# Attention: GpSimd multiplies and adds from ScalarE's copies, and the value products are placed three items apart

## The reference

```python
def _L0_attn_b_ref(x, w_in, w_out):
    # B = 4, L = 1024, E = 128, H = 16 heads, D = 8
    qkv = jnp.einsum('ble,fe->blf', x, w_in)
    q, k, v = to_heads(...)                       # [B, H, L, D]
    scores = jnp.einsum('bhqd,bhkd->bhqk', q, k) / sqrt(D) + alibi_bias(H, L)   # causal
    attn = jax.nn.softmax(scores, axis=-1)
    ctx = jnp.einsum('bhqk,bhkd->bhqd', attn, v)
    return jnp.einsum('ble,fe->blf', ctx, w_out)
x = x + _L0_attn_b_ref(_layernorm(x), w_in, w_out)
```

## Time and profile before

| | before |
|---|---|
| median of 3 runs | 1679.25 us (1678.73 to 1680.9) |
| the profiled execution's own time | 1676.88 us |
| its span in the profile | 1675.1 us |
| busy over the span: PE, DVE, ACT, POOL | 98%, 76%, 63%, 15% |
| attention, units 0 to 15 | 724.19 to 1128.87 us |
| one unit with g of 1 to 3 | 24.12 us |
| one unit with g = 0 (4, 8, 12) | 27.42 us |

### The profile page before, as it was taken

How to read it: one execution, slowest core, us unless ns; L and a number is a source line. 1 busy time by engine, 2 the same in 40 slices (tenths; PEclk the granted TensorE clock), 3 DMA queues, 4 the chain that set the end, 5 groups by cost and what they waited for, 6 DMA issues and landing times.

```text
span 1675.1 us, 28454 instructions
## 1 busy us (share of the span) xinstructions
PE 1636.6 (98%) x10387; PEld 1170.9 (70%) x10387; DVE 1272.8 (76%) x2541; ACT 1063.6 (63%) x1976; POOL 248.1 (15%) x469
## 2 busy tenths in 40 slices
PE   6999999999999999999999999999999999999998
PEld 4668787887778887754444544438888888888887
DVE  6789677776877777789999999946666666666665
ACT  6555765675566565578888888885555555555554
POOL 6522001200210113421211221220000000000000
PEclk9999999999999999999999999999999999999999
DMA  7000011002000023223212111100000000000000
GB/s 226 1 0 1 1 30 34 1 1 55 12 1 1 25 90 113 89 83 97 63 28 65 46 47 52 28 3 1 7 1 7 1 7 7 1 7 7 1 7 7
DMA packets 63446, 52.46 MB, mean 31 GB/s; under 512 B 7999, under 2 KB 58574, under 8 KB 63310
## 3 DMA queue, kind: packets, MB, share of 16 engines
q1 hardware_dynamic: 63136, 50.57, 10.4%
q10 hardware_dynamic: 174, 0.07, 0.0%
HBM read 32.40 MB, written 18.22 MB: 30 GB/s over the span
## 4 chain that ended last, share of the span: by engine, by line
PE 89%; DVE 6%; ACT 3%; issue 1%; POOL 0%; DMA 0%; DVEq 0%; SPq 0%; POOLq 0%
PE ps L1380 7%; PE ps L1417 7%; PE ps L1418 7%; PE ps L1419 7%; PE ps L1251 7%; PE ps L1252 6%; PE ps L1253 6%; PE ps L1196 6%; PE ps L933 4%; PE ps L1441 4%; PE ps L1442 4%; PE ps L1443 3%; PE ps L1267 3%; PE ps L1269 3%; PE ps L1268 3%; PE ps L1179 3%
## 5 line engine op out<-in xcount | busy, mean ns | idle before, releaser
L2392 DVE SCALAR_TENSOR_TENSOR hid<-sg,ps 128x512 f32<-128x512 f32 x256 | 175.7, 686 | 183.7 <-PE ps L1419 182.9
L1848 ACT ACTIVATE sg<-ps 128x512 f32<-128x512 f32 x256 | 153.3, 599 | 236.2 <-PE ps L1419 234.6
L1762 ACT ACTIVATE sg<-ps 128x512 f32<-128x512 f32 x256 | 153.4, 599 | 200.3 <-PE ps L1253 195.1
L2254 DVE TENSOR_TENSOR hid<-sg,ps 128x512 f32<-128x512 f32 x256 | 174.8, 683 | 136.9 <-PE ps L1253 95.8
L2244 DVE TENSOR_REDUCE negp<-ps 128x1 f32<-128x512 f32 (+2 forms) x450 | 243.3, 611 | 8.2 <-PE ps L1179 6.8
L1757 ACT ACTIVATE pr<-ps 128x512 f32<-128x512 f32 x384 | 206.4, 601 | 48.1 <-PE ps L1171 30.5
L1251 PE MATMUL ps<-xn_hi,w_hi 128*128 128x512 f32 x510 | 209.1, 410 | 0.0
L1417 PE MATMUL ps<-xn_hi,w_hi 128*128 128x512 f32 x512 | 202.5, 395 | 0.0
L1418 PE MATMUL ps<-xn_lo,w_hi 128*128 128x512 f32 x512 | 200.2, 391 | 0.0
L1252 PE MATMUL ps<-xn_lo,w_hi 128*128 128x512 f32 x510 | 199.8, 392 | 0.0
L1253 PE MATMUL ps<-xn_hi,w_lo 128*128 128x512 f32 x510 | 199.7, 392 | 0.0
(11 more groups left out here) (293 smaller groups left out, 3068.7 us busy)
## 6 DMA issues: line engine op xcount, KB each, us to landing
qs<-qd SPq DMA_DIRECT2D x60, 96.0 KB
ks<-kd SPq DMA_DIRECT2D x60, 96.0 KB
kd<-qkp SPq DMA_DIRECT2D x14, 256.0 KB, 2.9
qd<-qkp SPq DMA_DIRECT2D x7, 384.0 KB, 2.6
w_raw<-in_Wg SPq DMA_DIRECT2D x4, 512.0 KB, 7.3
w_raw<-in_Wu SPq DMA_DIRECT2D x4, 512.0 KB, 7.4
w_raw<-in_Wd SPq DMA_DIRECT2D x4, 512.0 KB, 8.9
work<-hd SPq DMA_DIRECT2D x8, 256.0 KB, 5.0
```

## The change

VectorE keeps only the reciprocal of each result, and now takes it from SBUF. ScalarE copies the transposed result from bank 7 to a new buffer `rt` (nine columns of each 32, so 144 per partition). GpSimd multiplies it into `ctxt`. In the units with g = 0 ScalarE also copies each projection from bank 7 to `yS`, and GpSimd adds that to x. Bank 7 is given free by ScalarE's copies. The last results and the last projections, those of unit 15 and sequence 3, stay with VectorE. The value products get other items, three apart where they were two to five apart, and transposes, copies and projections move with them.

```diff
-VALUES_AT = [10, 13, 15, 18, 23, 26, 29, 33, 35, 38]
+VALUES_AT = [11, 14, 18, 21, 24, 26, 29, 32, 38, 41]
...
-OWN_MAXIMA, BEFORE_T, NEXT_MAXIMA, OWN_T = 4, 7, 29, 32
-CONTEXT_T, PROJECT_OUT = (15, 21), (18, 26)
-BEFORE_OUT, OWN_COPY, PLACE, NEXT_COPY, OWN_OUT = 4, 5, 18, 29, 29
-CONTEXT_OUT = (15, 24)
+OWN_MAXIMA, BEFORE_T, NEXT_MAXIMA, OWN_T = 5, 8, 29, 35
+CONTEXT_T, PROJECT_OUT = (14, 24), (17, 27)
+BEFORE_OUT, OWN_COPY, PLACE, NEXT_COPY, OWN_OUT = 5, 6, 19, 29, 29
+CONTEXT_OUT = (14, 24)
+BEFORE_RESULT, OWN_RESULT = 9, 35
 BEFORE_NORM, OWN_NORM = 10, 35
-PROJECT_ADD = (18, 26)
+PROJECT_COPY = (17, 27)
...
+            def weighted_result(n, c):          # GpSimd
+                g0, at = n % NG * HG * HD, n * 2 + 1 - c
+                pool.wait_ge(T["onorm"], at + 1)
+                g.tensor_tensor(ctxt[...], rt[:, :, :, 0:HD], rl[:]...to_broadcast([P, SUB, HG, HD]),
+                                ALU.mult).then_inc(T["ctx"], 1)
+            def add_projection(b, u):           # GpSimd
+                pool.wait_ge(T["c_out"], projections_out(b, u))
+                g.tensor_tensor(rows, rows, yS[:], ALU.add).then_inc(T["xadd"], 1)
...
             for n in range(UNITS):
                 split_max(n * 2 + 1)
...
+                else:
+                    weighted_result(n - 1, 0)
                 for st in MASKED:
                     mask_step(n, st)
+                    if after_context and st == SUB:
+                        add_projection(b - 1, 0)
...
                         split_max(n * 2 + 2)
+                        if after_context:
+                            add_projection(b - 1, 1)
+                if n < LAST_UNIT:
+                    weighted_result(n, 1)
...
+                def result_to_tokens(n, c):     # ScalarE, after the exponential of item 9 or 35
+                    act.wait_ge(T["oT"], at + 1)
+                    a.copy(rt[:], bank(7)...[:, :, :, 0:HD + 1]).then_inc(T["o_out"], 1)
+                def projection_out(b, u):       # ScalarE
+                    act.wait_ge(T["proj"], b * 2 + u + 1)
+                    a.copy(yS[:], bank(7)).then_inc(T["c_out"], 1)
...
+                def reciprocals(n, c):          # VectorE, after the reduction of item 10 or 35
+                    dve.wait_ge(T["o_out"], tokens_out(at))
+                    v.reciprocal(rl[:], rt[:, :, :, HD]).then_inc(T["onorm"], 1)
...
-                            normalise(n - 1, 0)
-                        if g == 0 and n and k in PROJECT_ADD:
-                            add_projection(b - 1, PROJECT_ADD.index(k))
+                            reciprocals(n - 1, 0)
```

More of the change, by code:

```diff
@@ L129, in reduced_to, with results_out, tokens_out, contexts_out @@
     return EARLY_REDUCES + (n - 1) * REDUCES_TO[-1] + (REDUCES_TO[k] if k >= 0 else 0)
+def results_out(at):
+    return 2 * at + 1 if at < 2 * UNITS - 1 else 2 * at
+def tokens_out(at):
+    return 2 * at + 2
+def contexts_out(b, u):
+    return 4 * b + 2 * u + 1 if b < B - 1 else 4 * b + u + 1
+def projections_out(b, u):
+    return 4 * b + 2 * u + 2
 def jobs_done(n, k):
     return N_JOBS + (n - 1) * NG_S + k + 1
-VALUES_AT = [10, 13, 15, 18, 23, 26, 29, 33, 35, 38]
+VALUES_AT = [11, 14, 18, 21, 24, 26, 29, 32, 38, 41]
 for _sl, _at in enumerate(VALUES_AT):
@@ L433, in build @@
             rl = sb("rl", [P, SUB, HG], F32, two)
+            rt = sb("rt", [P, SUB, HG, HD + 1], F32, two)
         qkd = [nc.dram_tensor(n, (len(PAIRS), D, TOK), BF16, kind="Internal").ap() for n in ("qd", "kd")]
@@ L906, in mask_step @@
                                 pattern=[[0, HG], [1, HALF]], channel_multiplier=-1).then_inc(T["masked"], 1)
+            def weighted_result(n, c):
+                g0, at = n % NG * HG * HD, n * 2 + 1 - c
+                pool.wait_ge(T["onorm"], at + 1)
+                g.tensor_tensor(ctxt[:, c * SUB:(c + 1) * SUB, g0:g0 + HG * HD].rearrange("p t (h d) -> p t h d", h=HG),
+                                rt[:, :, :, 0:HD], rl[:].unsqueeze(3).to_broadcast([P, SUB, HG, HD]),
+                                ALU.mult).then_inc(T["ctx"], 1)
+            def add_projection(b, u):
+                pool.wait_ge(T["c_out"], projections_out(b, u))
+                rows = xs(b * BLK + u * SUB, SUB)
+                g.tensor_tensor(rows, rows, yS[:], ALU.add).then_inc(T["xadd"], 1)
             def norm_of_tile(t):
@@ L915, in _ @@
                     root_of_projected(LAST)
+                else:
+                    weighted_result(n - 1, 0)
+                b, after_context = n // NG, n and n % NG == 0
                 for st in MASKED:
                     mask_step(n, st)
+                    if after_context and st == SUB:
+                        add_projection(b - 1, 0)
                     if n == 0 and st == SUB + 1:
@@ L1392, in context_T @@
                     pe.wait_ge(T["ctx"], b * (2 * NG) + 2 * NG)
-                    if u == 1:
+                    if u == 1 and b < B - 1:
+                        pe.wait_ge(T["c_out"], projections_out(b, 0))
+                    if u == 1 and b == B - 1:
                         pe.wait_ge(T["xadd"], b * 2 + 1)
@@ L1398, in project_out @@
                 def project_out(b, u, to=7):
-                    pe.wait_ge(T["c_out"], b * 2 + u + 1)
+                    pe.wait_ge(T["c_out"], contexts_out(b, u))
                     for j in range(SUB):
@@ L1475, in project_last @@
                         w = slice(2 * D, 3 * D)
-                        pe.wait_ge(T["ctx"], 2)
+                        pe.wait_ge(T["o_out"], tokens_out(1))
                         for j in range(SUB):
@@ L1494, in unit @@
                             if n:
-                                pe.wait_ge(T["ctx"], n * 2 - 1)
+                                pe.wait_ge(T["o_out"], tokens_out(n * 2 - 2))
                             else:
@@ L1512, in unit @@
                             elif g == 0:
-                                pe.wait_ge(T["xadd"], b * 2)
+                                pe.wait_ge(T["c_out"], projections_out(b - 1, 1))
                             else:
-                                pe.wait_ge(T["ctx"], n * 2)
+                                pe.wait_ge(T["o_out"], tokens_out(n * 2 - 1))
                             if n == 1:
@@ L1835, in context_out @@
                     a.copy(ctxT[:], bank(at)).then_inc(T["c_out"], 1)
+                def result_to_tokens(n, c):
+                    at = n * 2 + 1 - c
+                    act.wait_ge(T["oT"], at + 1)
+                    if at:
+                        act.wait_ge(T["ctx"], at)
+                    a.copy(rt[:], bank(7).rearrange("p (t h w) -> p t h w", t=SUB, h=HG)[:, :, :, 0:HD + 1]
+                           ).then_inc(T["o_out"], 1)
+                def projection_out(b, u):
+                    act.wait_ge(T["proj"], b * 2 + u + 1)
+                    if b * 2 + u:
+                        act.wait_ge(T["xadd"], b * 2 + u)
+                    a.copy(yS[:], bank(7)).then_inc(T["c_out"], 1)
                 def input_out(t, at):
@@ L1890, in unit @@
                             place_values((n + 1) // NG, (n + 1) % NG)
+                        if k == BEFORE_RESULT and n:
+                            result_to_tokens(n - 1, 0)
+                        if g == 0 and n and k in PROJECT_COPY:
+                            projection_out(b - 1, PROJECT_COPY.index(k))
                         if g == 0 and n and k in CONTEXT_OUT:
@@ L1896, in unit @@
                             result_out(n, 1)
+                        if k == OWN_RESULT and n < LAST_UNIT:
+                            result_to_tokens(n, 1)
                         if k == LAST_INPUT and n == LAST_UNIT:
@@ L2338, in normalise @@
                     dve.wait_ge(T["oT"], at + 1)
+                    dve.wait_ge(T["ctx"], UNITS * 2 - 2)
                     v.reciprocal(rl[:], src[:, :, :, HD]).then_inc(T["onorm"], 1)
@@ L2347, in add_projection @@
                 def add_projection(b, u, at=7):
+                    dve.wait_ge(T["xadd"], TILES - 2)
                     dve.wait_ge(T["proj"], b * 2 + u + 1)
@@ L2448, in unit @@
                                 dve.wait_ge(G["third"], TILES * 2)
-                            normalise(n, 1)
+                            if n < LAST_UNIT:
+                                reciprocals(n, 1)
+                            else:
+                                normalise(n, 1)
                 def ffn_alone():
```

7 lines of the change are left out of this document (4 added, 3 removed).

## The result

The changed kernel takes 1669.72 us (median of 4 runs, 1668.14 to 1670.63), the kernel before 1678.99 beside it (4 runs): a ratio of 0.9945, 95% interval 0.9927 to 0.9962, or 9.3 us less. A second batch of five runs gave 1669.21 against 1678.87, ratio 0.9943 [0.9931, 0.9956].

What follows compares the result with a forecast made beforehand. VectorE was taken to set the pace in ten ordinary units. Terms 9.2 + 3.7 + 0.7 + 0.3 = 13.9 off 1676.88 gave 1663.0, plus 2.4 for the median 1665.4 us; range 1661.0 to 1673.0.

Steps and rivals of the forecast that it cites:

- the 0.66 a unit: VectorE, both results of a unit: 0.33 us removed between reciprocal and next reduction, twice, 0.66 in all.
- rival E: Slower: GpSimd late with the maxima's split if its multiplication takes 3 us or more; 1686 at 3.5 us; chance 0.05.
- Ten ordinary units: Units 2, 3, 5, 6, 7, 9, 10, 11, 13, 14: from 24.11 to 23.2 us, ten times 0.92, 9.2 in all.
- VectorE idles 0.1 at item 27 and nowhere else: In an ordinary unit under the new places, VectorE's only idle time is 0.1 us, giving a unit of 23.2.
- the walk: An ordinary unit followed item by item, each job no sooner than the reduction three before it: VectorE idle 0.1 us.
- rival B: TensorE or ScalarE takes VectorE's place in ordinary units: gain of 3 to 10 us, middle 7, 1672; chance 0.18.
- the maxima's way back: Maxima through DRAM into the queries, 3.2 us from ScalarE's copy to item 0: cost 0, up to 0.5 with g = 0.
- Units 4, 8, 12: Units with g = 0: from 27.42 to 26.2 us with VectorE idle about 3.05, saving 3.7 over three units.
- The 2.4 that was added for the median: The median of runs lies 2.4 us above the profiled execution, so 1663.0 became 1665.4.
- C (more): Units 4, 8 and 12 gain the full 1.86 each, the reciprocal costs 0.1: 18 us in all, 1661; chance 0.05.
- D (no difference): VectorE's saved time returns in full as idle time because TensorE sets the pace: 1676 to 1682; chance 0.06.
- the wait at item 35: VectorE waiting for ScalarE's copy at item 35: forecast cost 0, at most 0.3 us a unit; rival B allowed 0.3.

Runs made afterwards that it cites:

- the kernel without the trip: The changed kernel, loading for one half of the queries maxima stored two steps earlier, already in DRAM: 1666.38 us, ratio 0.9931 to the kernel before.
- the places alone: The kernel before with only the changed kernel's item constants, VectorE still multiplying and adding from bank 7: 1677.62 us, ratio 0.9997.
- the engines alone: The changed kernel with the old places for products, transposes and projections, result copies at items 8 and 34: 1675.91 us, ratio 0.9985 to the kernel before.
- the second profile: The changed kernel, unedited, measured and profiled a second time: 1669.21 us, ratio 0.9943 to the kernel before.

## Why the prediction was right, and where it was off

**VectorE's work, and the 0.66 a unit: right.** VectorE is busy 23.0 to 23.1 in a plain unit (forecast the same), 0.16 to 0.17 pass from the reciprocal to the next reduction (forecast 0.17). The reciprocal from SBUF lasts 0.253 in the median against the earlier trace rows's 0.249. The Trainium skill's fixed cost ("VectorE: DVE Perf Modes", errata section), by which it would have lost 65 ns, doesn't show in these medians: the measurement decides, and the 1.9 us it would have added aren't there.

**ScalarE and GpSimd: right.** By line and shape over the attention of the changed kernel (busy, mean ns, idle ahead):

```profile
L930 POOL TENSOR_TENSOR ctxt<-rt,rl 128x128 f32<-128x128 f32 x30 | 12.2, 406 | 89.1 <-DVE rl L2401 88.1
L938 POOL TENSOR_TENSOR x<-x,yS 128x512 f32<-128x512 f32 x6 | 7.6, 1271 | 4.4 <-ACT yS L1893 4.4
...
L1886 ACT COPY rt<-ps 128x144 f32<-128x144 f32 x30 | 8.6, 287 | 0.0
L1893 ACT COPY yS<-ps 128x512 f32<-128x512 f32 x6 | 3.5, 585 | 1.8 <-PE ps L1445 1.8
```

The multiplication takes 0.406 (forecast 0.46), the addition 1.27 (1.29), the copies 0.29 and 0.59 (0.27, 0.6). At the end of unit 4 the split ends 1.67 after the last reduction (857.42 to 859.09, forecast 1.87), and the multiplication ahead of it starts 0.27 after that reduction, so rival E had no ground. In units 0 to 14 VectorE never waits for a copy of ScalarE either (once in unit 15, where it has nothing else to do).

**Ten ordinary units: the largest term, 9.2 forecast, 3.8 came** (241.6 to 237.8 over the ten). Two steps of it failed.

First, "VectorE idles 0.1 at item 27 and nowhere else". It idles 0.33 there, and a plain unit is 23.49, not 23.2: 2.9 us over ten units, of which the 0.33, less the 0.1 that was forecast, is 2.3. The step was right in place and too small in size. Products at 24 and 26 are two items apart, and the walk gave the lead of TensorE too much at that point. Moving them to three apart removed the wait and gave 23.14. This is rival B in a small form: TensorE did take VectorE's place, at one item of 36.

Second, the maxima's way back. I had 3.2 for it against 4.5 in an ordinary unit, from the row of unit 6 alone, and wrote a cost only for units with g = 0. In units 3, 5, 9 and 10 it costs 1.0, 0.9, 0.8 and 0.3 (each against 23.49), and the ten units together take 237.8 against 234.9 in the kernel without the trip, so 2.9. Two things were missed. The margin of 1.3 was that of the old places. In unit 6 of the changed kernel the store is issued at 901.06 and the rows have landed at 904.18, 3.1 later as before. But the last product has moved from item 35 to 38, and the score of item 0 comes 3.3 behind the store (904.40) and no longer 4.5. A margin of 0.2 is left. VectorE's smaller work has no part in that: the places alone give the same 3.3, and the engines alone keep 4.5. And a store isn't always 1.4. It was 2.6 to 3.0 ahead of units 4, 6 and 11 of the kernel before too, where the margin hid all but some tenths of it; one row of one unit stood for a duration that goes up to twice as much. Of the 5.4 missing, these are 2.9 and 2.9, less 0.4 by which the kernel before stood above its plain 24.12 in units 10 and 11.

**Units 4, 8, 12: 3.7 forecast, 2.7 came.** 26.40, 26.42 and 26.84 against 26.2, with VectorE idle 3.1 to 3.4 for 3.05 (the waits that the forecast lists add up to 3.1). The places are about as forecast (unit 8 names 0.60, 0.64, 0.63, 0.33 and 0.84). Unit 12's 0.4 more goes with the store ahead of unit 13, one of the long ones (1.94, and 27.55 for the unit in the second profile, with 2.61).

**Ends.** Unit 1 gained 0.7, as forecast. Unit 0 lost 0.2 where 0.3 was to be gained. TensorE's granted clock is 0.89 in it and was 0.95: it stands at the lower level, 1.2 GHz, for 6.8 us and no longer 3.4. In both kernels it falls some 1.5 to 2 us behind a wait of TensorE of 0.8 (which ends at 732.58 in the changed kernel and at 731.10 before). The places alone have 32.17 us at 0.89, the engines alone 31.76 at 0.95, so this comes with the places. The forecast had no term for the clock. Unit 15 gained 0.2 where none was forecast.

The sum: 13.9 forecast; less 5.4, 1.0 and 0.5, plus 0.2, makes the 7.2 of the attention. The medians show 9.3. A profile is of one execution, and those of before and after stand on different sides of their medians; where the 2.1 between them lie no row tells.

**Luck in the number.** By its mechanism the forecast gave 1663.0 for the profiled execution, which came at 1670.39: 6.5 gained of 13.9, less than half. The 2.4 that was added for the median, because the profiled execution of before stood so far below its own, wasn't there after the change (the median is 0.7 below the profiled one). This error of 3.1 went the forecast's way. Had the median stood 2.4 above the profiled execution again, it would have been 1672.8, at the very edge of the range.

**Rivals.** C (more) and D (no difference) didn't come. B's 3 to 10 contains the result, and the forecast's own band (1661.5 to 1668.5) doesn't: it is the share of B in the range that takes it in. Of what B describes, the lost margin of TensorE was there at one place, the wait at item 35 wasn't. The mechanism that cost as much wasn't among the rivals at all.

## What to carry to other kernels

When steps of a hand-ordered pipeline move, list every transfer and handover that ends within the time to be gained, and take the slack from the new schedule: here 1.4 us of slack for a trip through DRAM became 0.2 by the new places alone. Take a DMA's duration from all its instances, not from one, and look at what else used the queues' engines in the slow ones. And when work is moved off an engine in a pipeline ordered by hand, expect to gain only where the other engine's places are moved as well: apart, the two halves gave 0.4 (no difference, by its interval) and 2.1 us here, and together 9.3.

## What was unexpected of the hardware

The loading of instructions disturbs small transfers. Where an instruction packet of 16 KB (q8, 0.9 to 1.7 us) began with a 12 KB store ahead of an item 0, the store took 1.9 to 3.4 us and not 1.37, in 58 cases of 58; with packets of 8 KB (q14) it took 1.36 to 2.5. In the changed kernel this happened ahead of five of fifteen units. The places moved when TensorE got more instructions far ahead of them. So adding or removing instructions anywhere earlier in a program can move time between stages that weren't touched (units 3 and 5 went from 24.53 and 24.40 to 23.48 and 23.49 by 128 idle waits hundreds of microseconds ahead), and a change of a few tenths in one unit is no evidence on an edit unless the stores beside it are looked at.

GpSimd's multiplication of 128x128 with one strided and one broadcast input took 0.406 us beside VectorE's 0.29 for the same elements: a factor of 1.4, where the 128x512 additions have 1.8 (1.27 against 0.69). The Trainium skill's advice against this move ("GPSIMD Engine Reference", Engine selection) holds for the time of one instruction, with 1.4 and 1.8 for its factor of two; here GpSimd was busy 5.6 of 23.5 us, and no engine waited for its multiplication.
